# Inverse standard deviation of the normalisations: one power on GpSimd in place of ScalarE's square root and the vector engine's reciprocal

## The chip, the cores and the metric

The kernel runs on one core of one Trainium2 chip. The metric is the device time of the core in microseconds, lower is better. Before the change the median of three runs is 2083.49 us (2082.4 to 2088.18).

## The reference

The program is a decoder of four layers with three sublayers each: attention, cross attention and feed-forward, on 4 x 256 tokens of 256 channels. The twelve sublayers are all different in kind (chunked linear attention, grouped-query cross attention with rotary positions, ternary feed-forward, a state-space model, and so on). Every sublayer ends in the same residual sum and normalisation:

```python
def _layernorm(x, axis=-1, eps=1e-05):
    m = jnp.mean(x, axis=axis, keepdims=True)
    v = jnp.var(x, axis=axis, keepdims=True)
    return (x - m) / jnp.sqrt(v + eps)

x = _layernorm(x + _L0_attn_ref(x, ...), axis=-1)
x = _layernorm(x + _L0_xattn_ref(x, ctx_2048, ...), axis=-1)
x = _layernorm(x + _L0_ffn_ref(x, ...), axis=-1)
...                                # twelve in all
```

## The kernel before, in words

The 1024 tokens lie on 128 partitions in eight tiles of 256 channels (`NT` = 8): `Y` holds the sum before a normalisation, `X` the normalised tiles with tokens on partitions, `XT` the same turned, channels on partitions. Each sublayer is a row of stages. A stage (`stage`, line 172) is a block in which each engine runs its own list of instructions, joined by semaphores; at its end GpSimd clears the stage's semaphores and all engines meet at a barrier (lines 180 and 181). Nothing of the next stage runs before that.

Ten of the twelve normalisations are stages of their own (`layer_norm`, line 302). The statistics of each tile (`stats`) are there already. The vector engine makes mean and variance of the eight tiles (`mv`, line 321), adds the epsilon (line 323) and signals `ln_var`. ScalarE takes the square root of the eight variances of each partition (line 335) and signals `ln_std`. The vector engine takes the reciprocal (line 325) and normalises tile by tile (line 327). TensorE turns the tiles (line 349) in four groups, each after four normalised tiles, and ScalarE copies them to `XT` (line 339). At the start of the stage ScalarE takes a root of a constant into `ln_one` (line 333), and where its function table is not the one with the root, the table load stands ahead of that instruction.

Two normalisations are fused into the last stage of their sublayer, the quantised cross attention of the third layer (`quantized_core`) and the RWKV attention of the fourth (line 2298), by the class `Finish` (line 3223). It works in two halves of four tiles: `variance(half)`, `root(half)` on ScalarE (line 3275), `normalise(half)` with the reciprocal on the vector engine (line 3282), `turn(half)` on TensorE, `store(half)` on ScalarE. The order in which these stand among the stage's other work is written out by hand on each engine.

The head RMS (`head_rms`, line 558) also takes a square root on ScalarE (line 573); it is used in the first sublayer and twice in the cross attention of the second layer. In the RWKV sublayer the exponential of the time decay (line 2385) is the first thing that ScalarE does, and the vector engine's first scan (line 2432) needs it and TensorE's first product.

Of the kernel before, what the change touches and what calls it, by code (L numbers as in the profile page):

```python
# [18 lines left out]
P = 128  # L19
B, S, D = 4, 256, 256  # L20
TOK = B * S
NT = TOK // P
# [5 lines left out]
ALU = mybir.AluOpType  # L28
# [17 lines left out]
def rows(v):  # L46

    v = np.asarray(v).reshape(1, -1)
    return np.broadcast_to(v, (P, v.shape[1]))
# [68 lines left out]
def shape_constants():  # L118
    p, j = np.arange(P)[:, None], np.arange(P)[None, :]
    f = np.float32  # L120
    inv_freq = (f(1.0) / np.power(f(10000.0), np.arange(0, P, 2, dtype=f) / f(P))).astype(f)
    return dict(
        ident=(p == j).astype(f),
        keep=(p <= j).astype(f),
        deny_q=np.where(j > p, f(NEG), f(0)),
        deny_k=np.where(p > j, f(-NEG), f(0)),
        third=((p % 32 == np.arange(32)[None, :]) & (p < 96)).astype(f),
        eighth=(p // 16 == np.arange(8)[None, :]).astype(f),
        inv_freq=rows(inv_freq), ones=np.ones((P, P), f),
        rank=rows(np.arange(16, 0, -1).astype(f)))  # L130


def pack(parts):
# [168 lines left out]
def layer_norm(g, weights=None, out=None):  # L302
# [5 lines left out]
    with ExitStack() as ctx:  # L308
        sb, pb = places(g, ctx)
        st = g.stats  # L310
        mv = sb("ln_mv", [P, NT, 2])
        root_of_one = sb("ln_one", [P, 1])
        ps = [pb(f"ln_ps{i}", [P, 4, P]) for i in range(4)]
        with stage(g, "ln_var ln_std ln_chain ln_x ln_turned") as (
                block, var_ready, std_ready, chain_sem, x_ready, turned):

            @block.vector
            def _(dve):
                link = Count(dve, chain_sem)
                for t in range(NT):  # L320
                    last = nc.vector.bn_aggr(mv[:, t, :], st[:, t, :])
                link(last)
                nc.vector.tensor_scalar(mv[:, :, 1], mv[:, :, 1], LN_EPS, None, ALU.add).then_inc(var_ready, 1)
                dve.wait_ge(std_ready, 1)
                link(nc.vector.reciprocal(mv[:, :, 1], mv[:, :, 1]))  # L325
                for t in range(NT):
                    nc.vector.tensor_scalar(X[:, t, :], Y[:, t, :], mv[:, t, 0:1], mv[:, t, 1:2],  # L327
                                            ALU.subtract, ALU.mult).then_inc(x_ready, 1)

            @block.scalar  # L330
            def _(act):

                nc.scalar.activation(root_of_one[:, :], g.ones[:, 0:1], ACT.Sqrt)  # L333
                act.wait_ge(var_ready, 1)
                nc.scalar.activation(mv[:, :, 1], mv[:, :, 1], ACT.Sqrt).then_inc(std_ready, 1)  # L335
                if out is None:
                    for i in range(4):
                        act.wait_ge(turned, i + 1)
                        nc.scalar.copy(XT[:, i % 2, (i // 2) * 512:(i // 2) * 512 + 512],
                                       ps[i][:, :, :].rearrange("p a b -> p (a b)"))  # L340

            if out is None:
                @block.tensor
# [1539 lines left out]
def quantized_core(g, qT, kT, vi, sq, wp, ahead, weights):  # L1883
# [8 lines left out]
    with ExitStack() as ctx:  # L1892
# [8 lines left out]
        with stage(g, "qc_scored qc_max qc_bias qc_exp qc_turned0 qc_turned1 qc_turned2 qc_turned3 qc_turned4 qc_turned5 qc_used qc_recip "  # L1901
# [6 lines left out]
            @block.gpsimd  # L1908
            def _(pool):
                for i in range(ahead.count):  # L1910
                    ahead.compare(i, ahead_compared, ahead_made)
                pool.wait_ge(ahead_made, ahead.count)

            @block.sync
            def _(sp):
# [104 lines left out]
            def _(act):  # L2020
# [12 lines left out]
                                         scale=sq[:, t, h:h + 1], accum_out=sm[:, i:i + 1]).then_inc(exped, 1)  # L2033
                for t in range(NT):
                    store_turned(t)
                fin.root(0)
                fin.store(0)
                fin.root(1)
                fin.store(1)


# [256 lines left out]
def L3_attn(g, W, weights):  # L2298
# [8 lines left out]
    with ExitStack() as ctx:  # L2307
# [11 lines left out]
        with stage(g, "dm_kproduct dm_vrproduct dm_wexp dm_signs dm_highest dm_diff dm_arg dm_exps dm_vstored dm_gate "  # L2319
# [41 lines left out]
            def _(act):  # L2361
# [25 lines left out]
                for hf in range(2):  # L2387
# [2 lines left out]
                        store_v(hf, m)  # L2390
                    exponents(2 * hf + 1)
                    gates(hf)
                fin.root(0)
                fin.store(0)
                fin.root(1)
                fin.store(1)

            @block.gpsimd
            def _(pool):
# [7 lines left out]
                def weigh_before(u):  # L2407
                    pool.wait_ge(qsum, 2 * u + 2)
                    nc.gpsimd.tensor_tensor(eq[:, u], ea[:, u], before(q, u), ALU.mult).then_inc(before_weighted, 1)
# [6 lines left out]
                for hf in range(2):  # L2416
                    weigh(2 * hf)
                    weigh_before(2 * hf)
                    weigh(2 * hf + 1)
                    weigh_before(2 * hf + 1)  # L2420
                    weigh_gate(2 * hf)
                    weigh_gate(2 * hf + 1)

            @block.vector
            def _(dve):
# [797 lines left out]
class Finish:  # L3223
# [45 lines left out]

    def root(self, half):  # L3270

        nc = self.g.nc
        v = self.mv[:, 4 * half:4 * half + 4, 1]
        nc.scalar.wait_ge(self.var, half + 1)
        nc.scalar.activation(v, v, ACT.Sqrt).then_inc(self.std, 1)

    def normalise(self, half):

        nc, g, mv = self.g.nc, self.g, self.mv
        v = mv[:, 4 * half:4 * half + 4, 1]  # L3280
        nc.vector.wait_ge(self.std, half + 1)
        self.link(nc.vector.reciprocal(v, v))
        for t in range(4 * half, 4 * half + 4):
            nc.vector.tensor_scalar(g.X[:, t, :], g.Y[:, t, :], mv[:, t, 0:1], mv[:, t, 1:2], ALU.subtract,
                                    ALU.mult).then_inc(self.x, 1)
# [259 lines left out]
def program(nc, a, out, parts, spans, const_at, first=0, last=11):  # L3545
    g = Core()
    g.nc = nc
    with ExitStack() as ctx:
# [15 lines left out]
        g.inv_freq = const("inv_freq")  # L3564
        g.ones = const("ones")
        g.rank = const("rank")
        keep3 = sb("keep3", [P, 3, P])
        g.keep3 = keep3[:, :, :]
        ident_b = sb("ident_b", [P, P], BF16)
# [106 lines left out]
```

## Time and profile before

| | |
|---|---|
| median of 3 runs | 2083.49 us |
| profiled execution | 2080.46 us, span 2078.5 us |
| TensorE matmul busy | 1657.9 us, 80% of the span |
| vector engine busy | 1342.2 us, 65% |
| ScalarE busy | 1061.7 us, 51% |
| GpSimd busy | 575.4 us, 28% |
| mean granted TensorE clock | 0.863 |

The shares are averages over some fifty stages with different limits. In the normalisation stages no engine is busy with anything else, so they are read by their order in time, instruction by instruction. Times in the rows are microseconds from the start of the span.

### The profile page before, as it was taken

How to read it: one execution, taken by the hardware profiler on the slowest of the kernel's cores; microseconds unless marked ns; L12 is line 12 of the kernel's file. 1: busy time of each engine (PE TensorE's matmuls, PEld its weight loads, DVE VectorE, ACT ScalarE, POOL GpSimd, SP SyncE). 2: the span in 40 equal slices, each digit the busy share in tenths (PEclk: the TensorE clock that was granted, in tenths of full speed). 3: DMA queues.
4: the chain of work that ended last, by engine and by line, in shares of the span. 5: the costliest groups of instructions: out<-in, count | busy, mean ns of one | idle time of the engine just before them, and what ended most of it. 6: DMA issues, size and time to landing. Idle time of an engine off the chain costs nothing. (4 is left out here: it accounts for less than half of the span.)

```text
span 2078.5 us, 28504 instructions
## 1 busy us (share of the span) xinstructions
PE 1657.9 (80%) x9533; PEld 1039.9 (50%) x9541; DVE 1342.2 (65%) x2664; ACT 1061.7 (51%) x2191; POOL 575.4 (28%) x466
## 2 busy tenths in 40 slices
PE   7957999999997879998399579772899767457924
PEld 3743566666775536656266357451222434226712
DVE  4767777676664448883676456246999747825467
ACT  2024555565543248893188158324899621515525
POOL 0406341322100029890320000012990000406710
PEclk9989999999999989999699779896555669777958
DMA  4000000000001001110000000015999700020000
GB/s 199 27 1 26 1 1 1 1 1 1 1 1 43 16 32 42 51 41 16 0 2 2 26 1 2 23 77 136 162 182 184 123 21 5 0 81 1 2 0 21
DMA packets 163007, 80.65 MB, mean 39 GB/s; under 512 B 155280, under 2 KB 156432, under 8 KB 161200
## 3 DMA queue, kind: packets, MB, share of 16 engines
q1 hardware_dynamic: 162720, 78.46, 15.8%
q8 instruction: 77, 1.26, 0.3%
q14 instruction: 66, 0.54, 0.1%
q10 hardware_dynamic: 144, 0.39, 0.0%
HBM read 39.44 MB, written 1.11 MB: 20 GB/s over the span
## 5 line engine op out<-in xcount | busy, mean ns | idle before, releaser
L1213 POOL TENSOR_TENSOR ss_u<-dx,b_rows 128x512 f32<-128x512 f32 x128 | 159.0, 1273 | 242.3 <-POOLq L181 226.3
L2032 ACT ACTIVATE qc_p<-qc_s,qc_bias,sq 128x1024 int16<-128x1024 f32 x128 | 154.1, 1204 | 16.9 <-DVE qc_bias L1999 6.8
L1295 DVE TENSOR_TENSOR_SCAN ss_h<-ss_decay,ss_u 128x512 f32<-128x512 f32 x128 | 146.5, 1204 | 24.2 <-PE ss_ht L1253 18.4
L932 ACT ACTIVATE gq_p<-gq_s,gq_bias,gq_rq 128x512 f32<-128x512 f32 x128 | 98.5, 773 | 119.0 <-DVE gq_bias L1002 118.9
L1997 DVE TENSOR_REDUCE qc_mx<-qc_s 128x1 f32<-128x1024 f32 x128 | 155.4, 1214 | 3.8 <-PE qc_s L1932 3.8
L865 POOL TENSOR_TENSOR gq_xw<-gq_x,weights 128x512 f32<-128x512 f32 x48 | 67.9, 1414 | 295.1 <-ACT gq_x L892 294.5
L1932 PE MATMUL qc_s<-kT,qT 64*128 64x512 bf16 x256 | 130.8, 618 | 13.6 <-ACT qc_p L2032 7.3
L1267 PE MATMUL ss_acc<-ss_hc,consts 128*128 128x512 f32 x256 | 130.9, 594 | 0.0
L800 PE MATMUL gq_s<-gq_KT,gq_QT 128*128 128x512 f32 x256 | 121.5, 597 | 3.7 <-ACT gq_p L932 3.7
L822 PE MATMUL gq_o<-gq_pT,gq_V 128*128 128x256 f32 x512 | 121.2, 379 | 1.4 <-DVE gq_pT L1036 1.4
L999 DVE TENSOR_REDUCE gq_mx<-gq_s 128x1 f32<-128x512 f32 x128 | 88.3, 691 | 43.5 <-PE gq_s L800 43.1
L822 PEld LDWEIGHTS gq_o<-gq_pT,gq_V 128*128 128x128 f32 x512 | 94.2, 190 | 24.3 <-issue 12.5
L1253 PEld LDWEIGHTS ss_ht<-consts,ss_h 128*128 128x128 f32 x512 | 64.7, 143 | 79.4 <-issue 52.8
L1036 DVE COPY gq_pT<-gq_t 128x512 f32<-128x512 f32 x64 | 44.3, 692 | 86.6 <-PE gq_t L810 86.6
L1223 ACT ACTIVATE ss_decay<-delta,ss_A 128x510 f32<-128x510 f32 x128 | 87.8, 686 | 16.7 <-DVE ss_h L1295 15.7
L349 PE MATMUL ln_ps<-consts,X 128*128 128x128 f32 x144 | 32.7, 420 | 79.2 <-DVE X L327 79.2
L779 PE MATMUL gq_item<-weights,XT 128*128 128x512 f32 x192 | 91.4, 597 | 4.2 <-ACT gq_x L892 2.1
L1231 ACT ACTIVATE ss_hc<-ss_ht,bct 128x512 f32<-128x512 f32 x128 | 86.8, 678 | 7.8 <-PE ss_ht L1253 7.6
L1942 PEld LDWEIGHTS qc_o<-vi,qc_pT 128*128 128x128 f16 x1024 | 37.8, 106 | 105.9 <-issue 65.2
L1472 ACT ACTIVATE bc_w<-bc_s 128x512 f32<-128x512 f32 x128 | 72.4, 597 | 32.3 <-PE bc_s L1413 30.5
L1253 PE MATMUL ss_ht<-consts,ss_h 128*128 128x128 f32 x512 | 78.1, 276 | 12.2 <-DVE ss_h L1295 11.7
L3442 POOL MEMSET qi_ks<- 128x512 bf16 x2 | 1.0, 524 | 299.9 <-POOLq L181 299.9
(576 smaller groups left out, 4127.1 us busy)
## 6 DMA issues: line engine op xcount, KB each, us to landing
b_rows<-b_rows SPq DMA_DIRECT2D x16, 512.0 KB, 3.6
weights<-in_weights SPq DMA_DIRECT2D x1, 6152.0 KB, 17.7
weights<-in_weights SPq DMA_DIRECT2D x1, 5248.0 KB, 16.7
weights<-in_weights SPq DMA_DIRECT2D x1, 3072.0 KB, 10.4
weights<-in_weights SPq DMA_DIRECT2D x1, 2156.0 KB, 7.4
qc_pT<-qc_p SPq DMA_TRANSPOSE x128, 3.3
weights<-in_weights SPq DMA_DIRECT2D x1, 1410.0 KB, 9.0
weights<-in_weights SPq DMA_DIRECT2D x1, 1282.0 KB, 6.2
```

The lines of the kernel that those rows point to most:

```text
L779: last = nc.tensor.matmul(pj[:, :], src[:, k, t * P:t * P + P], w[:, k, :], start=(k == 0), stop=(k == 1))
L800: nc.tensor.matmul(sc[t][:, :], QT[:, u, t * P:t * P + P], KT[b % 2][:, u // 4, :], start=True, stop=True).then_inc(scored, 1)
L822: last = nc.tensor.matmul(po[:, :], V[b % 2][:, k, u // 4 * P:u // 4 * P + P], prT[c % 2][:, k, :], start=(k == 0), stop=(k == 3))
L932: nc.scalar.activation(pr[c % 2][:, t, :], sc[t][:, :], ACT.Exp, bias=bias[:, c, t:t + 1], scale=rq[b % 2][:, t, u:u + 1], accum_out=sm[:, ...
L999: nc.vector.tensor_reduce(mx[:, c, t:t + 1], sc[t][:, :], AX.X, ALU.max, negate=True).then_inc(maxed, 1)
L1213: nc.gpsimd.tensor_tensor(u_in[i % 3][:, :], dx[:, m, hf * HT:hf * HT + HT], rows.rows[c % 2][:, n % rows.NEACH, :], ALU.mult).then_inc(in ...
L1253: last = nc.tensor.transpose(ht[k % 2][:, m * P:m * P + P], h[group % 2][:, m, t * P:t * P + P], g.ident)
L1267: nc.tensor.matmul(acc[t][:, :], g.ident, hc[k % 3][:, :], start=False, stop=(n == NS - 1)).then_inc(summed, 1)
L1295: nc.vector.tensor_tensor_scan(h[group % 2][:, m, :], decay[i % 2][:].rearrange("p b t -> p (b t)"), u_in[i % 3][:, :], 0.0, ALU.mult, ALU ...
L1932: last = nc.tensor.matmul(sc[u % 3][:, n * 512:n * 512 + 512], qT[e, t, h // 2, :], kT[e, 4 * n:4 * n + 4, h // 2, :], start=True, stop=True)
L1997: nc.vector.tensor_reduce(mx[:, i:i + 1], sc[i % 3][:, :], AX.X, ALU.max, negate=True).then_inc(maxed, 1)
L2032: nc.scalar.activation(pi[i % R][:, :], sc[i % 3][:, :], ACT.Exp, bias=bias[:, i:i + 1], scale=sq[:, t, h:h + 1], accum_out=sm[:, i:i + 1] ...
```

## The change

The root and the reciprocal are replaced by one instruction on GpSimd: the variances to the power of a constant -0.5, which is a new column of the constants. ScalarE's dummy root and its root go, and so do the reciprocals of the normalisations. In the two fused normalisations the root moves to GpSimd's list.

```diff
@@ shape_constants
-        rank=rows(np.arange(16, 0, -1).astype(f)))
+        rank=rows(np.arange(16, 0, -1).astype(f)), neg_half=np.full((P, 1), -0.5, f))
@@ layer_norm
                 dve.wait_ge(std_ready, 1)
-                link(nc.vector.reciprocal(mv[:, :, 1], mv[:, :, 1]))
                 for t in range(NT):
...
             @block.scalar
             def _(act):
-
-                nc.scalar.activation(root_of_one[:, :], g.ones[:, 0:1], ACT.Sqrt)
-                act.wait_ge(var_ready, 1)
-                nc.scalar.activation(mv[:, :, 1], mv[:, :, 1], ACT.Sqrt).then_inc(std_ready, 1)
...
+            @block.gpsimd
+            def _(pool):
+                pool.wait_ge(var_ready, 1)
+                nc.gpsimd.tensor_tensor(mv[:, :, 1], mv[:, :, 1], g.neg_half.to_broadcast([P, NT]),
+                                        ALU.pow).then_inc(std_ready, 1)
@@ quantized_core, GpSimd
                 pool.wait_ge(ahead_made, ahead.count)
+                fin.root(0)
+                fin.root(1)
@@ quantized_core and the RWKV attention, ScalarE
-                fin.root(0)
                 fin.store(0)
-                fin.root(1)
                 fin.store(1)
@@ the RWKV attention, GpSimd
                     weigh_before(2 * hf + 1)
+                    if hf == 1:
+                        fin.root(0)
                     weigh_gate(2 * hf)
                     weigh_gate(2 * hf + 1)
+                fin.root(1)
@@ Finish
     def root(self, half):
...
-        nc.scalar.wait_ge(self.var, half + 1)
-        nc.scalar.activation(v, v, ACT.Sqrt).then_inc(self.std, 1)
+        nc.gpsimd.wait_ge(self.var, half + 1)
+        nc.gpsimd.tensor_tensor(v, v, g.neg_half.to_broadcast([P, 4]), ALU.pow).then_inc(self.std, 1)
     def normalise(self, half):
...
-        self.link(nc.vector.reciprocal(v, v))
```

ScalarE at the second normalisation (behind the grouped-query cross attention of the first layer), before; `ln_mv` holds mean and variance, `ln_ps` the turned tiles:

```order
L330 UNCONDITIONAL_BRANCH
L333 ACT_TABLE_LOAD
L333 ACTIVATE ln_one<-consts 128x1
L335 ACTIVATE ln_mv<-ln_mv 128x8
L339 COPY XT<-ln_ps_132 128x512
```

The same place after, on ScalarE:

```order
L328 UNCONDITIONAL_BRANCH
L333 COPY XT<-ln_ps_130 128x512
L333 COPY XT<-ln_ps_131 128x512
L333 COPY XT<-ln_ps_132 128x512
L333 COPY XT<-ln_ps_133 128x512
```

And on GpSimd, which had only its semaphore clears there:

```order
L180 ISA x29
L336 UNCONDITIONAL_BRANCH
L339 TENSOR_TENSOR ln_mv<-ln_mv,consts 128x8
L177 UNCONDITIONAL_BRANCH
L180 ISA x13
```

The table load, the dummy root and the root are gone from ScalarE; the power stands alone on GpSimd.

ScalarE at the start of the RWKV attention, before (`dm_w` is the exponential of the time decay, `dm_d` a difference that the vector engine makes):

```order
L2360 UNCONDITIONAL_BRANCH
L2385 ACT_TABLE_LOAD
L2385 ACTIVATE dm_w<-weights 128x2
L2377 ACTIVATE dm_arg_476<-dm_d,dm_wn 128x512
L2378 ACTIVATE dm_a_467<-dm_arg_476 128x512
```

And after:

```order
L2360 UNCONDITIONAL_BRANCH
L2385 ACTIVATE dm_w<-weights 128x2
L2377 ACTIVATE dm_arg_468<-dm_d,dm_wn 128x512
L2378 ACTIVATE dm_a_459<-dm_arg_468 128x512
```

The load ahead of the exponential is gone, since the table of the exponential is still in place from the sublayers before.

GpSimd in the second half of the RWKV attention, before (`dm_no` is the numerator, `dm_r` the gate):

```order
L2403 TENSOR_TENSOR dm_bv<-dm_b_468,dm_v 128x512
L2405 TENSOR_TENSOR dm_v<-dm_eb,dm_v 128x512
L2409 TENSOR_TENSOR dm_eq<-dm_ea,dm_q 128x512
L2414 TENSOR_TENSOR dm_no<-dm_no,dm_r 128x512 x2
L177 UNCONDITIONAL_BRANCH
```

And after, with the two powers (`fi_mv`):

```order
L2401 TENSOR_TENSOR dm_bv<-dm_b_460,dm_v 128x512
L2403 TENSOR_TENSOR dm_v<-dm_eb,dm_v 128x512
L2407 TENSOR_TENSOR dm_eq<-dm_ea,dm_q 128x512
L3276 TENSOR_TENSOR fi_mv<-fi_mv,consts 128x4
L2412 TENSOR_TENSOR dm_no<-dm_no,dm_r 128x512 x2
L3276 TENSOR_TENSOR fi_mv<-fi_mv,consts 128x4
```

The first power stands ahead of the two gate products, the second behind them. Over the whole program ScalarE has 39 table loads before and 28 after: twelve go (six of line 333, two of line 3275, and those of lines 1585, 1856, 2032 and 2385), and one comes, ahead of the root of the first head RMS in the second layer's cross attention (line 573).

## Rows read from the trace of the kernel before

**Rows 1.** The waits of all engines: us in total, times, longest.

```profile
PE ln_ps L349 <- DVE X L327: 79.2, 9, 30.6
```

**Rows 2.** Order of time, normalisation without table load: start, us, engine, what.

```profile
149.77 0.17 DVE L323 TENSOR_SCALAR ln_mv<-ln_mv 128x8 f32<-128x8 f32 x1
...
150.46 2.67 DVE L327 TENSOR_SCALAR X<-Y,ln_mv 128x256 f32<-128x256 f32 x8
```

**Rows 3.** Order of time, normalisation with table load.

```profile
650.44 1.28 ACT L333 ACT_TABLE_LOAD   x1 [5.77 <-PEq L181]
...
651.15 0.17 DVE L323 TENSOR_SCALAR ln_mv<-ln_mv 128x8 f32<-128x8 f32 x1
651.74 0.20 ACT L333 ACTIVATE ln_one<-consts 128x1 f32<-128x1 f32 x1
...
652.31 2.67 DVE L327 TENSOR_SCALAR X<-Y,ln_mv 128x256 f32<-128x256 f32 x8
```

**Rows 4.** Line 333 on ScalarE: ns min, median, max, first and last start.

```profile
L333 ACT ACTIVATE ln_one<-consts x10: 202/203/203, 149.1 to 2071.2; 128x1 f32<-128x1 f32 x10
L333 ACT ACT_TABLE_LOAD  x6: 1283/1283/1283, 650.4 to 2069.9; - x6
```

**Rows 5.** GpSimd's groups (busy us, mean ns of one), then its first two-input instruction.

```profile
L1213 POOL TENSOR_TENSOR ss_u<-dx,b_rows 128x512 f32<-128x512 f32 x128 | 159.0, 1273 | 242.3 <-POOLq L181 226.3 <-DVE ss_h L1295 16.0
...
L2629 POOL TENSOR_TENSOR mn_h<-mn_h,weights 128x256 f32<-128x256 f32 x8 | 5.7, 748 | 27.1 <-ACT mn_sq L2635 27.1
...
L3443 POOL TENSOR_TENSOR X<-X,weights 128x2048 f32<-128x2048 f32 x1 | 3.8, 3811 | 0.0
...
L3668 POOL MEMSET const-float32-1.0<- 128x1 f32 x1 | 0.1, 98 | 0.0
...
159.54 1.09 POOL L865 TENSOR_TENSOR gq_xw<-gq_x,weights 128x512 f32<-128x512 f32 x1 [67.81 <-ACT gq_x L892]
```

**Rows 6.** Order of time, RWKV attention: hand-overs from and to GpSimd.

```profile
1771.19 1.27 POOL L2403 TENSOR_TENSOR dm_bv<-dm_b,dm_v 128x512 f32<-128x512 f32 x1 [211.11 <-ACT dm_v L2366]
...
1772.50 3.27 DVE L2444 TENSOR_TENSOR_SCAN dm_p<-dm_a,dm_bv 128x256 f32<-128x256 f32 x2 [3.10 <-POOL dm_bv L2403]
...
1783.61 0.69 DVE L2452 TENSOR_TENSOR dm_no<-dm_no,dm_v 128x512 f32<-128x512 f32 x1
...
1784.45 1.58 POOL L2414 TENSOR_TENSOR dm_no<-dm_no,dm_r 128x512 f32<-128x512 f32 x1 [3.90 <-DVE dm_no L2452]
```

**Rows 7.** Order of time, first half of the normalisation in the quantised attention.

```profile
1650.62 0.17 DVE L3268 TENSOR_SCALAR fi_mv<-fi_mv 128x4 f32<-128x4 f32 x1
...
1651.69 0.42 DVE L365 BATCH_NORM_STATS2 stats<-Y 128x6 f32<-128x256 f32 x1
...
1653.24 1.38 DVE L3284 TENSOR_SCALAR X<-Y,fi_mv 128x256 f32<-128x256 f32 x4
```

**Rows 8.** Order of time, first half of the normalisation in the RWKV attention.

```profile
1813.43 3.35 DVE L2455 RECIPROCAL dm_eq<-dm_eq 128x512 f32<-128x512 f32 x1
1816.82 0.18 DVE L3282 RECIPROCAL fi_mv<-fi_mv 128x4 f32<-128x4 f32 x1
```

**Rows 9.** Order of time, its second half.

```profile
1831.86 0.17 DVE L3268 TENSOR_SCALAR fi_mv<-fi_mv 128x4 f32<-128x4 f32 x1
...
1832.52 1.38 DVE L3284 TENSOR_SCALAR X<-Y,fi_mv 128x256 f32<-128x256 f32 x4
```

**Rows 10.** Order of time, start of the RWKV attention.

```profile
1761.25 1.28 ACT L2385 ACT_TABLE_LOAD   x1 [0.85 <-PEq L181]
...
1761.29 2.81 PE L2334 MATMUL dm_k<-XT,weights 128*128 128x512 f32 x6 [1.51 <-PEq L181]
...
1763.35 1.26 DVE L2432 TENSOR_TENSOR_SCAN dm_o<-dm_w,dm_k 128x256 f32<-128x256 f32 x2
```

**Rows 11.** Order of time, first head RMS of the second layer's cross attention.

```profile
1002.42 2.56 ACT L571 ACTIVATE rms_sq<-q 128x256 f32<-128x256 f32 x8 [1.87 <-PEq L181]
...
1005.94 0.42 ACT L573 ACTIVATE rms_ms<-rms_ms 128x256 f32<-128x256 f32 x1 [0.96 <-DVE rms_ms L583]
```

**Rows 12.** Order of time, ScalarE's first exponential in the quantised attention, behind its load.

```profile
1458.89 1.20 ACT L2032 ACTIVATE qc_p<-qc_s,qc_bias,sq 128x1024 int16<-128x1024 f32 x1 [1.31 <-DVE qc_bias L1999]
```

More of the change, by code:

```diff
@@ L311, in layer_norm @@
         mv = sb("ln_mv", [P, NT, 2])
-        root_of_one = sb("ln_one", [P, 1])
         ps = [pb(f"ln_ps{i}", [P, 4, P]) for i in range(4)]
@@ L2392, in _ @@
                     gates(hf)
-                fin.root(0)
                 fin.store(0)
-                fin.root(1)
                 fin.store(1)
@@ L3270, in root @@
     def root(self, half):
-        nc = self.g.nc
+        nc, g = self.g.nc, self.g
         v = self.mv[:, 4 * half:4 * half + 4, 1]
-        nc.scalar.wait_ge(self.var, half + 1)
-        nc.scalar.activation(v, v, ACT.Sqrt).then_inc(self.std, 1)
+        nc.gpsimd.wait_ge(self.var, half + 1)
+        nc.gpsimd.tensor_tensor(v, v, g.neg_half.to_broadcast([P, 4]), ALU.pow).then_inc(self.std, 1)
     def normalise(self, half):
@@ L3566, in program @@
         g.rank = const("rank")
+        g.neg_half = const("neg_half")
         keep3 = sb("keep3", [P, 3, P])
```

## The prediction

> **What bounds the kernel now.** I read four views in this order. First the waits: TensorE waits 79.2 us in nine standing-alone normalisations for the normalised tiles X [rows 1]. Nothing else runs in such a stage, so every tenth of a microsecond between the variance and the first normalise instruction is a tenth of the total. Second the order of time inside such a stage. Without a table load, the vector engine adds the epsilon from 149.77 to 149.94, ScalarE takes the root, the vector engine the reciprocal, and the first normalise starts at 150.46: a gap of 0.52 us [rows 2]. With a table load, the load runs from 650.44 to 651.72, the dummy root follows at 651.74, and the gap from 651.32 (end of the epsilon add) to 652.31 is 0.99 us [rows 3]: the load starts with the stage, and all but 0.47 us of it and of the dummy root lies beside the bn_aggr work. Six of the ten stages have the load [rows 4], four have not. Third the GpSimd rows, for the price of what replaces the pair [rows 5], and the hand-overs from and to GpSimd [rows 6]. Fourth the places where a table load stood or will stand outside these stages [rows 7 to 12].
>
> **The change, term by term.** Let G be the new gap: hand-over to GpSimd, one pow, hand-over back. GpSimd starts 0.15 us after the vector instruction it waits for (1784.30 to 1784.45), and the vector engine 0.04 us after GpSimd (1772.46 to 1772.50) [rows 6]. So G = pow + 0.19.
>
> 1. Ten standing-alone stages: 10 G - (4 x 0.52 + 6 x 0.99) = 10 G - 8.02 us [rows 2 to 4].
> 2. The second half of each fused normalisation, where the engines wait in the same way: 1831.86 + 0.17 = 1832.03 to 1832.52 is 0.49 us, and the other one is the same in kind: 2 G - 0.98 us [rows 9].
> 3. The first half in the quantised attention: the epsilon add ends at 1650.79, ScalarE first finishes copies, then loads the table, and the normalise starts at 1653.24, 2.45 us later. The vector engine has adds and statistics of its own until 1651.69 + 0.42 = 1652.11 [rows 7]. With the pow it starts at 1652.14 if G is under 1.35: -1.10 us. TensorE has the turn of these tiles and then the last projection behind it, so it is on the path. If G is over 1.35 the gain shrinks by the difference. GpSimd's own list there is comparisons of the next sublayer's weights, with the two roots behind them.
> 4. The first half in the RWKV sublayer: the vector engine computes a quotient meanwhile and reaches its small reciprocal at 1816.82, straight from a reciprocal of 3.35 us of that quotient. Only the small one goes: 0.18 + 0.03 = -0.21 us [rows 8]. On GpSimd the gate products are now queued behind the root, which waits for the variance. They need the numerator, for which the vector engine has two instructions of 0.69 us behind the variance [rows 6], so a pow of up to about 1.2 us holds nothing up, and a dearer one still has the 3.35 us as slack. I cost it at nothing.
> 5. Start of the RWKV sublayer: ScalarE's exponential table need not be loaded again, since nothing has displaced it. The load runs from 1761.25 and the vector engine waits for the exponential behind it, so that its first scan starts at 1763.35. TensorE's first product is two matmuls of a row of six in 2.81 us, so there by about 1762.3; the scan can then start at about 1762.35: -1.00 us, between -1.28 (the whole load) and 0 (if ScalarE's later chain absorbs it) [rows 10].
> 6. One load is added: the first head RMS of the second layer's cross attention found the root table in place and now doesn't. Its squares end at 1004.98, its root starts at 1005.94; a load of 1.28 us set off at 1004.98 ends at 1006.26: +0.33 us, between 0 and +1.28 [rows 11].
> 7. Loads at three other stage starts go too. ScalarE waits 1.31 us for the vector engine behind one of them [rows 12]; I cost all three at nothing, since what covers them is the first scores and maxima of the stage; without that cover they would be worth up to 1.28 us each.
> 8. The constants grow by one column of 760; I cost it at nothing.
>
> Sum: 12 G - 8.02 - 0.98 - 1.10 - 0.21 - 1.00 + 0.33 = 12 G - 10.98 us. Break-even is G = 0.915, a pow of 0.73 us.
>
> **The price of the pow.** The trace has no pow on any engine. From below: the shortest GpSimd row of all, a memset of one column, 0.10 us; then G = 0.29 and the sum is -7.5 us. A multiply costs 748 ns for 256 columns and 1273 ns for 512, that is 2.05 ns a column over a fixed 0.22 us, so eight columns at a multiply's price are 0.24 us, G = 0.43, sum -5.8 us [rows 5]. From above: the dearest GpSimd row, 3.81 us; G = 4.0, sum +37.0, and +39.7 with the 2.65 us that term 3 loses. I take the row nearest in kind and size, the two-input operation on 256 columns: 0.75 us. That leaves 0.53 us for eight columns of pow above the fixed part; that is 66 ns a column, some thirty times a multiply; nothing in the trace supports this figure more closely, so both ends stay in the range. G = 0.94 and the sum is +0.3 us. The profiled execution took 2080.46 us and would take 2080.8; it lies 3.03 us under the median of the three runs, and carried over to that median the forecast is 2083.8 us.
>
> **Two rules weighed.** The load costs 1.28 us here and the next activation starts 0.02 us behind it [rows 3]. The Trainium skill (ScalarE: Activation LUTs, What ACT_TABLE_LOAD costs) charges a drain of 1.38 us on top, 2.66 us for each switch. By that rule eleven loads fewer would be worth some 29 us (an estimate from that page), and the forecast would be 2055; the trace does not agree, because no such drain follows the load and most loads are covered.
>
> The first two-input instruction on GpSimd of the whole program, at 159.54, takes 1.09 us, less than the 1.27 us of a later group of the same shape, so no first use shows in this trace [rows 5]. The Trainium skill (GPSIMD Engine Reference, Instruction dispatch) says that the first call into a freshly loaded library kernel costs about 6 us without an instruction to show for it. If pow were such a kernel, the first normalisation would carry it once and the forecast would be 6 us later (an estimate from that page). No run here shows it so far.
>
> **The rivals.**
> - *Cheap pow.* The pow costs less than 0.4 us; at a multiply's price the sum is -5.8 us, 2077.7, at the floor -7.5 us, 2076.0. For it: the operand is eight columns. Against it: pow is no multiply; on the vector engine a reciprocal of 512 columns is 3.35 us where other two-input work on it is 0.69 [rows 6, 8], so division-like functions cost several times the plain ones even there.
> - *Dear pow, the rival on the other side.* A new wait takes the place of the removed one: in all ten stages and both second halves, the vector engine, and TensorE behind it, wait for GpSimd. It decides from G = 0.915, and passes 0.3% (6.25 us) from G = 1.43, a pow of 1.24 us. At a pow of 1.8 us the sum is 12 x 2.0 - 10.98 + 0.65 = +13.7 us, 2097.2; at the dearest GpSimd row 2123.2. For it: nothing in the trace bounds a transcendental function on this engine, and none of its rows is one. Against it: its rows here of 1 to 512 columns take 0.10 to 1.58 us [rows 5, 6].
> - *The covered loads were on the path after all.* With the three of term 7 in full, 3 x 1.28 = 3.8 us more gain: 2080.0. Against it: ScalarE's wait behind the load [rows 12].
> - *A first pow that is dear once.* The first normalisation waits for it, at the most as long as the dearest GpSimd row, 3.81 us: 2087.6. For it: pow stands nowhere in the program before. Against it: the first multiply's 1.09 us [rows 5].
> - *The change does nothing it says.* Against it: the order of ScalarE's instructions in the changed kernel has 28 table loads for 39, and no root in a normalisation.
>
> **How the numbers follow.** 0.3% is about what a measurement of this kernel tells from no change. Pow between 0.4 and 1.24 us, sum from -3.9 to +6.2: 0.53. Cheap pow: 0.20, of which 0.14 beyond 0.3%. Dear pow: 0.24, half of it over +22 us. Covered loads on the path: 0.02. A first pow dear once: 0.01. So faster 0.14, same 0.53 + 0.06 + 0.02 + 0.01 = 0.62, slower 0.24. The range runs from the floor of the pow, 2083.5 - 7.5 = 2076, to a G of 2.7 (12 x 2.7 - 10.98 + 1.35 = +22.8), 2106; half of the dear case and little else is left out.
>
> **What would show it.** In the profile after: ten pow rows of eight columns and four of four; their mean is the whole question, and the gap between the epsilon add and the first normalise should be that mean plus 0.19. All ten stages should have the same gap, where they now have 0.52 or 0.99. In the quantised attention the first normalise should follow the statistics directly at 0.03 us; the RWKV sublayer's first scan should come 1.0 us earlier after the stage's start; the head RMS should show a load that ends 0.3 us late. I am wrong in size if the mean pow is outside 0.4 to 1.24 us, and wrong in mechanism if the gap in a stage differs from pow plus 0.19 by over 0.2 us, or if stages without a normalisation change by over 1 us.

## The result: the changed kernel is 1.1% slower, beyond the range

| | before | after |
|---|---|---|
| median (range) of 4 runs each on one chip | 2085.84 us (2082.40 to 2088.18) | 2108.92 us (2104.58 to 2109.90) |
| profiled execution, its span | 2080.46, 2078.5 us | 2109.90, 2108.0 us |
| mean granted TensorE clock | 0.863 | 0.852 |

The ratio after to before is 1.0108, with an interval of 1.0085 to 1.0131. By the medians that is 23.1 us. The forecast was 2083.8, and the time lies 2.9 us above the top of the range. Three of the kernels below each have one execution far outside the rest (2409, 3399 and 4307 us); the ratios leave it out, the medians keep it and move by less than 0.2 us.

**The price of the power.** The groups of the two tiles in the changed kernel (engine, operation, count, then the shortest, median and longest in ns, first and last start):

```profile
L322 DVE TENSOR_SCALAR ln_mv<-ln_mv x10: 171/172/173, 153.5 to 2099.4; 128x8 f32<-128x8 f32 x10
L339 POOL TENSOR_TENSOR ln_mv<-ln_mv,consts x10: 1634/1637/1667, 153.8 to 2099.6; 128x8 f32<-128x8 f32 x10
...
L3276 POOL TENSOR_TENSOR fi_mv<-fi_mv,consts x4: 1007/1026/1389, 1671.5 to 1853.0; 128x4 f32<-128x4 f32 x4
```

Eight columns take 1.64 us and four 1.01 us: about 0.16 us a column over a fixed 0.4 us. The forecast had taken 0.75 us for eight. The wait of TensorE for the normalised tiles, 79.2 us before [rows 1], is now

```profile
PE ln_ps L349 <- DVE X L325: 88.3, 9, 31.8
```

The same stage as in [rows 3], in order of time after the change:

```profile
658.16 0.17 DVE L322 TENSOR_SCALAR ln_mv<-ln_mv 128x8 f32<-128x8 f32 x1
658.41 1.67 POOL L339 TENSOR_TENSOR ln_mv<-ln_mv,consts 128x8 f32<-128x8 f32 x1 [115.18 <-DVE ln_mv L322]
660.11 2.67 DVE L325 TENSOR_SCALAR X<-Y,ln_mv 128x256 f32<-128x256 f32 x8 [1.78 <-POOL ln_mv L339]
```

The gap is 1.78 us where it was 0.99; it is 1.75 to 1.78 us in all ten stages, against 0.52 or 0.99 before. Over the ten stages that adds 17.6 - 8.0 = 9.6 us. This is well short of 23.1 us.

**Where a large part of the rest went.** The third normalisation and the first product of the stage behind it show it. `ln_ps` are the sixteen turns of the normalised tiles, `si_x` the projection that follows, and ScalarE's line 3144 (3145 after) the first to read what it makes, its first consumer. Before, in order of time:

```profile
699.64 2.67 DVE L327 TENSOR_SCALAR X<-Y,ln_mv 128x256 f32<-128x256 f32 x8
701.08 3.67 PE L349 MATMUL ln_ps<-consts,X 128*128 128x128 f32 x16 [5.03 <-DVE X L327]
...
706.26 4.10 PE L3084 MATMUL si_x<-XT,weights 128*128 128x512 f32 x9 [1.51 <-PEq L181]
708.25 0.69 ACT L3144 ACTIVATE xc<-si_x,weights 128x512 f32<-128x512 f32 x1 [2.88 <-PE si_x L3084]
```

After:

```profile
708.40 2.68 DVE L325 TENSOR_SCALAR X<-Y,ln_mv 128x256 f32<-128x256 f32 x8 [1.75 <-POOL ln_mv L339]
709.83 3.68 PE L349 MATMUL ln_ps<-consts,X 128*128 128x128 f32 x16 [6.26 <-DVE X L325]
...
715.03 5.28 PE L3085 MATMUL si_x<-XT,weights 128*128 128x512 f32 x7 [1.52 <-PEq L181]
718.82 0.69 ACT L3145 ACTIVATE xc<-si_x,weights 128x512 f32<-128x512 f32 x1 [4.69 <-PE si_x L3085]
```

The turns take 3.67 us in both, and both stages need 5.2 us from the first turn to the first matmul behind. But the same product then takes 1.99 us before and 3.79 us after. The windows cut at these times (length, busy time of TensorE with its instructions, granted clock as a share of full speed, DMA share, GB/s), first before, then after:

```profile
706.26:708.25 1.99, 1.99 (x5) 1.00 0.49 107
```

```profile
715.03:718.82 3.79, 3.79 (x5) 0.50 0.65 207
```

The same five matmul records run at 2.4 GHz before and at 1.2 GHz after. TensorE had stood still before the turns for 5.03 us before and 6.26 us after; in these rows nothing else about its work differs. The Trainium skill (TensorE: Matmul & The Clock Gate, HAM oscillation) describes bursts of matmuls parted by waits that start again at the lower clock, at a price of half the throttled time. The trace agrees in size: 1.80 us of 3.79.

I read this time, from the first matmul behind a normalisation to its first consumer, in the eight stages where it can be told, in every kernel that follows. It is 1.99 to 2.08 us at the full clock and 3.4 to 3.9 at the lower one (the fourth stage has a shorter product, 1.14 or 2.08). The ninth is 2.58 us in every profile, and behind the tenth there is nothing. I call a product at the lower clock a slow product. Before, one of the eight is slow (the fifth, 3.46 us); after, seven (all but the second): 3.79, 1.99, 3.79, 2.08, 3.79, 3.70, 3.86 and 3.62 us. The eight add up to 9.9 us more than before.

### The profile page after: what moved, and what is told of

Its sections match the earlier page's. It is cut to its first block and busy times, and to the rows that moved or that the text cites. A ratio compares the mean times of both kernels' runs of the same rounds, so it can differ in the third digit from the quotient of the medians.

```text
span 2108.0 us, 28469 instructions
## 1 busy us (share of the span) xinstructions
PE 1677.4 (80%) x9533; PEld 1047.9 (50%) x9541; DVE 1338.9 (64%) x2650; ACT 1043.4 (49%) x2156; POOL 596.2 (28%) x480
## 3 DMA queue, kind: packets, MB, share of 16 engines
q8 instruction: 78, 1.28, 0.2%
## 5 line engine op out<-in xcount | busy, mean ns | idle before, releaser
L339 POOL TENSOR_TENSOR ln_mv<-ln_mv,consts 128x8 f32<-128x8 f32 x10 | 16.4, 1644 | 724.1 <-DVE ln_mv L322 724.1
L2034 ACT ACTIVATE qc_p<-qc_s,qc_bias,sq 128x1024 int16<-128x1024 f32 x128 | 154.2, 1204 | 21.5 <-DVE qc_bias L2001 11.4
L333 ACT COPY XT<-ln_ps 128x512 f32<-128x512 f32 x36 | 21.1, 586 | 139.1 <-PE ln_ps L349 139.1
## 6 DMA issues: line engine op xcount, KB each, us to landing
weights<-in_weights SPq DMA_DIRECT2D x1, 5248.0 KB, 16.7
```

The costliest lines, as they stand in the source:

```text
L2034: nc.scalar.activation(pi[i % R][:, :], sc[i % 3][:, :], ACT.Exp, bias=bias[:, i:i + 1], scale=sq[:, t, h:h + 1], accum_out=sm[:, i:i + 1] ...
```

## The experiments

In all of them theory A is that the longer standstill of TensorE leaves the stage behind at the lower clock. Its rivals were that the tiles or the constants had moved (B), that the new order of the queues or the absent table loads cost (C), and that the gaps alone account for the time (D). The texts of expectation speak of nine products; of these, eight can be told apart. The number after each ratio is the change of the median against the runs of the kernel before on the same chip.

**const_only.** The kernel before with the new column of the constants, which nothing reads.

```diff
-        rank=rows(np.arange(16, 0, -1).astype(f)))
+        rank=rows(np.arange(16, 0, -1).astype(f)), neg_half=np.full((P, 1), -0.5, f))
```

> The kernel before with the extra column of constants alone; nothing reads it, and all that follows it lies 32 bytes further on. Theory A (what is lost beyond the sum of the gaps is TensorE's granted clock behind longer pauses): same as before, 2083 to 2088 us. Rival B (the move of the tiles, or the larger load of constants, costs time of itself): up to 15 us slower, about 2100, with the first projection behind 36 us late by 1.5 us as in the changed kernel.

Measured 2083.77 us, ratio 0.9999 (0.9984 to 1.0014), -0.4 us; one slow product of eight. The constants cost nothing, and B falls as far as they go.

**cheap_mult.** The kernel after with everything where the change puts it, but the power is a multiply of the same size; the inverse deviation is left out and a constant stands for it.

```diff
-                nc.gpsimd.tensor_tensor(mv[:, :, 1], mv[:, :, 1], g.neg_half.to_broadcast([P, NT]),
-                                        ALU.pow).then_inc(std_ready, 1)
+                nc.gpsimd.tensor_tensor(mv[:, :, 1], g.ones[:, 0:NT], g.neg_half.to_broadcast([P, NT]),
+                                        ALU.mult).then_inc(std_ready, 1)
```

> The changed kernel with the power replaced by a multiply of two constants on the same 8 or 4 columns, so the standard deviation is left out of the result (a constant -0.5 takes its place); every wait, queue and removed table load is that of the change. It shows what the change would be worth if the power were cheap. By the sum of my prediction (multiply 0.24 us, gap 0.43) -5.8 us, 2077 to 2080. Theory A: at or below that, with the clock back at 0.86. Rival C (the moved order on the queues or the absent table loads cost the time, not the power's length): it stays near 2100 to 2108.

Measured 2078.20 us, ratio 0.9969 (0.9955 to 0.9982), -5.9 us; two slow products. Its row for the instruction:

```profile
L339 POOL TENSOR_TENSOR ln_mv<-consts x10: 200/202/204, 151.7 to 2069.2; 128x8 f32<-128x8 f32 x10
```

With 0.20 us the gap is 0.32 us. The forecast's sum at a multiply's price was -5.8 us, and that the two agree is in part luck: at the measured gap the sum is 12 x 0.32 - 10.98 = -7.1 us, and 1.0 us of it, the load at the RWKV start, was never to be had (term 5 below). Tiles, constants, queues and loads are all as in the kernel after, so B and C fall: the whole loss hangs on how long the power takes.

**paused and paused_mid.** The kernel before, root and reciprocal in place. In the ten normalisation stages the vector engine also waits for an addition of 690 (400) columns on GpSimd that starts with the variance.

```diff
+            @block.gpsimd
+            def _(pool):
+                pool.wait_ge(var_ready, 1)
+                nc.gpsimd.tensor_tensor(filler[:, :], ...[:, 0:690], ...[:, 0:690], ALU.add).then_inc(filled, 1)
...
                 link(nc.vector.reciprocal(mv[:, :, 1], mv[:, :, 1]))
+                dve.wait_ge(filled, 1)
```

> The kernel before, whole and with its table loads, but in the ten normalisation stages the vector engine also waits for a GpSimd addition of 690 columns (about 1.64 us by 2.05 ns a column over 0.22) that starts when the variance is there, so that the gap is about 1.8 us as in the changed kernel. Gaps alone: 10 x 1.8 - 8.0 = +10 us, 2095. Theory A (longer pauses also cost clock in the stage behind): +20 to +30 us, 2104 to 2112. Rival D (the extra loss belongs to something else in the change): +10 us, no more.

> The kernel before, paused as in the longer one but by an addition of 400 columns, about 1.04 us, so that the gap in all ten normalisation stages is about 1.24 us (0.52 or 0.99 before, 1.83 in the longer pause). Gaps alone: 10 x 1.24 - 8.0 = +4.4 us, 2088. Theory A (the clock behind the stage depends on the pause): between +4 and +14 us, with three to seven of the nine first products behind a normalisation slow (3.4 to 3.8 us to the first copy instead of 2.0). Rival D (gaps alone): 2088, with two of nine slow as before.

The filler of 690 columns is as long as the power:

```profile
L321 POOL TENSOR_TENSOR ln_filler<-Y x10: 1636/1637/1639, 152.1 to 2096.4; 128x690 f32<-128x690 f32 x10
```

paused: 2105.00 us, ratio 1.0094 (1.0071 to 1.0117), +20.9 us, seven slow products. Its gaps are 1.83 us, so they add 18.3 - 8.0 = 10.3 us by themselves. paused_mid: 2098.89 us, ratio 1.0070 (1.0050 to 1.0090), +15.1 us, four slow products; its gaps of 1.22 us add 4.2 us. The second is 1 us above what theory A had allowed it (+4 to +14). D falls: both lose some 11 us more than their gaps. In the profile of paused the eight first products hold 9.7 us of that. In the profile of paused_mid they hold only 4.9 of 10.9 us, so there more than half is not located. The third stage's product in paused, with the same columns of the windows as above:

```profile
715.98:719.77 3.79, 3.79 (x5) 0.50 0.66 210
```

No power, no absent load and no new column is in this kernel. The wait alone makes most of the loss of the kernel after (20.9 of 23.1 us).

**after_warm and before_warm.** TensorE turns the identity into a spare buffer twelve times at the start of the normalisation stages, once in the kernel after and once in the kernel before. The nine stages in which TensorE has turns are concerned.

```diff
                 def _(pe):
+                    for j in range(12):
+                        nc.tensor.transpose(spare[:, j % 4, :], g.ident, g.ident)
```

> The changed kernel, and in each normalisation stage TensorE turns the identity twelve times into a spare bank before it waits for the normalised tiles, so that it is busy for 1.3 to 2.6 us of the pause. Theory A: the granted clock behind the normalisations is high and 10 to 20 us come back, 2088 to 2098. Rival D: no change, 2105 to 2110, or slower by what the twelve overshoot.

> The kernel before with the twelve turns of the identity on TensorE at the start of each normalisation stage. Theory A: the two of nine slow first products of the kernel before become fast and the turns inside the stages run faster, 5 to 12 us gain, 2072 to 2079. Rival: the clock is high enough there already and the turns overshoot, 2084 to 2088.

after_warm: 2089.96 us, ratio 1.0021 (1.0008 to 1.0033), +5.8 us, two slow products; the gaps are still 1.75 to 1.78 us. before_warm: 2076.93 us, ratio 0.9972 (0.9956 to 0.9988), -6.8 us, no slow product. It is the fastest of all kernels here. Its third normalisation:

```profile
695.76 1.15 PE L347 MATMUL ln_spare<-consts 128*128 128x128 f32 x9
...
698.21 1.09 PE L352 MATMUL ln_ps<-consts,X 128*128 128x128 f32 x8 [1.30 <-DVE X L328]
...
699.50 1.09 PE L352 MATMUL ln_ps<-consts,X 128*128 128x128 f32 x8 [0.20 <-DVE X L328]
```

Each half of the turns now runs in 1.09 us, where all sixteen took 3.67 at the lower clock. From the first normalise instruction to the first matmul of the next stage it takes 5.39 us for 6.62. Turns faster than at the lower clock are found in five of the nine stages of after_warm and eight of before_warm, and this is a gain that the kernel before had to get as well. So the extra turns do not only undo what the change did, and the fair comparison is between the two warm kernels: the change costs 5.8 + 6.8 = 12.7 us there by the medians (10.2 by the ratios), against 23.1 (22.5) without the turns. So some 10 to 12 us of the loss exist only without those turns; the intervals of the three ratios leave this uncertain by some 6 us.

**split_pow.** The kernel after, with mean, epsilon and power in two halves of four tiles, so that the first power runs beside the second half of the means.

```diff
+                for hf in range(2):
+                    for t in range(4 * hf, 4 * hf + 4):
+                        last = nc.vector.bn_aggr(mv[:, t, :], st[:, t, :])
+                    link(last)
+                    v = mv[:, 4 * hf:4 * hf + 4, 1]
+                    nc.vector.tensor_scalar(v, v, LN_EPS, None, ALU.add).then_inc(var_ready, 1)
                 for t in range(NT):
+                    if t % 4 == 0:
+                        dve.wait_ge(std_ready, t // 4 + 1)
```

> The changed kernel, but in the ten normalisation stages mean, variance and power go in two halves of four tiles, so that the first power starts after four aggregations and takes about 1.0 us instead of 1.64. The last aggregation lies beside it. Gap from the end of all aggregations to the first normalise about 0.5 us instead of 1.77; the pause of TensorE is 1.2 us shorter. Gaps alone against the changed kernel: -12 us, 2096. Theory A: clock comes back as well, 2080 to 2092. Rival D: 2096.

Measured 2086.01 us, ratio 1.0008 (0.9994 to 1.0021), +2.2 us; two slow products. From the last of the epsilon additions to the first normalise instruction it is 0.63 to 0.67 us. Its second normalisation:

```profile
650.26 0.38 DVE L321 BATCH_NORM_AGGREGATE ln_mv<-stats 128x2 f32<-128x6 f32 x4 [2.64 <-PEq L181]
...
650.93 2.17 POOL L346 TENSOR_TENSOR ln_mv<-ln_mv,consts 128x4 f32<-128x4 f32 x2 [114.72 <-DVE ln_mv L324]
...
652.00 1.38 DVE L328 TENSOR_SCALAR X<-Y,ln_mv 128x256 f32<-128x256 f32 x4 [0.66 <-POOL ln_mv L346]
```

The power still costs 2 x 1.0 us, but one of them lies beside work, and nearly all of the loss is gone.

**split_warm and before_warm20.** Ten turns in split_pow, and twenty in place of twelve in the kernel before.

```diff
+                    for j in range(10):          # split_warm; range(20) in before_warm20
+                        nc.tensor.transpose(spare[:, j % 4, :], g.ident, g.ident)
```

> The changed kernel with mean, variance and power in two halves, and ten turns of the identity on TensorE at the start of each normalisation stage. Split alone gave 2086 with two of nine first products slow. Theory A: those two and the turns inside the stages become fast, 2070 to 2078, at or under the kernel before with its twelve turns (2077). Rival: the turns overshoot the shorter pause and give nothing, 2084 to 2088.

> The kernel before with twenty turns of the identity instead of twelve. With the clock high they take 2.2 us, with it low 4.3 us, against a pause of 2.8 to 3.3 us inside the stage. Theory A allows a small further gain where the clock is high (2074 to 2077) and a loss where it is low, up to 1 us a stage (2085).

split_warm: 2086.75 us, ratio 1.0021 (1.0008 to 1.0033), +4.2 us; it missed its expectation. Ten turns left the normalisation's own turns slow in the eight stages (6.38 to 6.64 us from the first normalise to the next stage's first matmul; 5.39 where they are fast), so they bought nothing; only one product of eight was slow. Its profile also begins with a slow stretch at 38 us, ahead of any normalisation. before_warm20: 2081.13 us, ratio 0.9999 (0.9986 to 1.0012), -1.5 us, no slow product. In its third stage the twenty turns run on until 700.9 us:

```profile
696.95 3.98 PE L347 MATMUL ln_spare<-consts 128*128 128x128 f32 x20 [2.23 <-PEq L181]
700.77 1.91 PE L352 MATMUL ln_ps<-consts,X 128*128 128x128 f32 x16
```

The normalisation's sixteen turns stand behind them in one block, where before_warm had started the first eight as soon as four tiles were there. By the same reading as for before_warm (normalisation stages and the products behind them) the twenty turns gain 8.3 us where the twelve gain 10.5, so their late end accounts for 2.2 of the 5.3 us between the two; where the rest is isn't shown.

**fused_only.** The kernel before with only the two fused normalisations changed (the lines of the diff in `Finish`, `quantized_core` and the RWKV attention).

```diff
-        nc.scalar.activation(v, v, ACT.Sqrt).then_inc(self.std, 1)
+        nc.gpsimd.tensor_tensor(v, v, g.neg_half.to_broadcast([P, 4]), ALU.pow).then_inc(self.std, 1)
...
-        self.link(nc.vector.reciprocal(v, v))
```

> The two fused normalisations changed (powers on GpSimd), the ten standing-alone stages as before. By the rows of the changed kernel: the first half in the quantised attention starts 1.2 us earlier, both second halves wait 0.65 us longer each, the rest cancels: 0 +- 1 us. Theory A: 2081 to 2086, same as before, since no long pause of TensorE is added. Rival C (the order on the GpSimd queue in the fused stages costs time): over 2090.

Measured 2083.81 us, ratio 1.0008 (0.9996 to 1.0020), +1.2 us. The loss is in the ten stages that stand alone. One thing speaks against reading too much into a single trace: this one has four slow products, though the code of its standing-alone stages is that of the kernel before. (The eighth has one table load more, since the quantised attention no longer takes a root, and a gap of 0.99 us for 0.52; its product is one of the four.) The profile is of an execution of 2087.26 us, the second longest of ten.

**pow_sizes.** Powers and multiplies of several sizes on GpSimd, behind the last normalisation.

```diff
+                    for op, ns in ((ALU.pow, (1, 2, 4, 8, 16, 32, 64, 128)), (ALU.mult, (1, 8, 32, 128))):
+                        for n in ns:
+                            nc.gpsimd.tensor_tensor(probe[:, n0:n0 + n], g.ones[:, 0:n],
+                                                    g.neg_half.to_broadcast([P, n]), op)
```

> The changed kernel with eight powers of 1 to 128 columns and four multiplies of 1 to 128 columns on GpSimd behind the last normalisation, for their durations. From 1.01 us at 4 columns and 1.64 at 8: 0.16 us a column over 0.39 us, so 20 us at 128 columns, if the price is linear; a multiply about 0.2 us at 1 to 8 columns. The rival reading is a fixed price with steps, under 5 us at 128.

One execution, 2141.70 us. The group (shortest, median, longest in ns):

```profile
L346 POOL TENSOR_TENSOR ln_probe<-consts x12: 183/1044/20719, 2094.3 to 2138.4; 128x1 f32<-128x1 f32 x2, 128x8 f32<-128x8 f32 x2, 128x32 f32<-128x32 f32 x2, 128x128 f32<-128x128 f32 x2
```

The longest, 20.72 us, is the power of 128 columns: (20.72 - 1.64) / 120 = 0.16 us a column, as between four and eight. The base was one here and the variance in the kernel, so the price does not hang on the data as far as these two go.

Up to its last normalisation the code of pow_sizes is that of the kernel after but for one spare tile, so its profile is a second look at that kernel. Six of its eight products are slow, and they are not the same ones: the third and the fifth are fast there, the second is slow. Its second stage, ahead of the feed-forward's first product (`ff_ps`):

```profile
659.66 3.67 PE L357 MATMUL ln_ps<-consts,X 128*128 128x128 f32 x16 [8.55 <-DVE X L326]
...
664.85 19.38 PE L1138 MATMUL ff_ps<-XT,weights 128*128 128x512 f32 x40 [1.52 <-PEq L181]
...
668.64 0.60 ACT L1148 ACTIVATE ff_r<-ff_ps 128x512 f32<-128x512 f32 x1 [4.69 <-PE ff_ps L1138]
```

TensorE stands still for 8.55 us before the turns, as in the kernel after. There the product took 1.99 us, here 3.79.

## Why the prediction was wrong, point by point

The time by the forecast's own sum with what was measured, in us of the profiled executions:

| step | forecast | measured |
|---|---|---|
| price of eight columns of pow | 0.75 (0.10 to 3.81) | 1.64 |
| hand-overs | 0.19 | 0.12 |
| 1: ten stages | 10 G - 8.02 = +1.4 | +9.6 |
| 2: second halves, fused | 2 G - 0.98 = +0.9 | +1.3 |
| 3: first half, quantised | -1.10 | -1.22 |
| 4: first half, RWKV | -0.21 | -0.22 |
| 5: load at the RWKV start | -1.00 | 0 |
| 6: load ahead of the head RMS | +0.33 | +0.34 |
| 7, 8: covered loads, constants | 0 | 0 |
| TensorE's clock behind the stages | not there | +9.9 |

Without the last row the measured terms make +9.8 us, and the time would have been some 2093 us, inside the range. **Two steps failed.** The first is the price of the pow, a term that was mis-sized. The forecast went by the nearest row in kind and size and ended at 66 ns a column where 157 were measured; it had called this figure weakly supported, and the dear rival (chance 0.24) stated this part rightly, the wait for GpSimd and its sign. The second weighs more, and no rival had it: "12 G" priced a longer gap at one microsecond per microsecond, and the clock of TensorE behind it at nothing. In the kernel before TensorE's turns already run at 1.2 GHz, but in seven of eight stages the clock is back at 2.4 GHz as the next stage begins. With 0.8 to 1.2 us more of standstill it is, in most stages, back only about the end of the first product, and that product costs up to 1.8 us more. At a pow of 1.8 us the forecast said 2097.2; the runs gave 2108.9 at 1.64. Of its three signs of being wrong two came true: the mean pow lies outside 0.4 to 1.24 us, and stages without a normalisation changed by over 1 us. A third step, term 5, failed by 1.0 us (below).

**Hand-overs and gaps.** GpSimd starts 0.08 us after the epsilon addition and the vector engine 0.03 us after GpSimd. The gap is the pow plus 0.12, within the 0.2 us that the prediction set for its mechanism, and alike in all ten stages, as it said.

**Term 2.** The last half of the RWKV attention after the change, which answers to [rows 9]:

```profile
1852.78 0.17 DVE L3269 TENSOR_SCALAR fi_mv<-fi_mv 128x4 f32<-128x4 f32 x1
1853.03 1.01 POOL L3276 TENSOR_TENSOR fi_mv<-fi_mv,consts 128x4 f32<-128x4 f32 x1 [10.57 <-DVE fi_mv L3269]
1854.07 1.38 DVE L3284 TENSOR_SCALAR X<-Y,fi_mv 128x256 f32<-128x256 f32 x4 [1.12 <-POOL fi_mv L3276]
```

A gap of 1.12 us for 0.49. The term took the price of eight columns for four, which would have been too much at the true price.

**Term 3** was right. The quantised attention after the change, which answers to [rows 7]:

```profile
1671.47 1.03 POOL L3276 TENSOR_TENSOR fi_mv<-fi_mv,consts 128x4 f32<-128x4 f32 x1 [90.41 <-DVE fi_mv L3269]
...
1672.22 0.42 DVE L365 BATCH_NORM_STATS2 stats<-Y 128x6 f32<-128x256 f32 x1
1672.55 0.72 DVE L3284 TENSOR_SCALAR X<-Y,fi_mv 128x256 f32<-128x256 f32 x2
```

From the start of the last statistics to the first normalise it is 0.33 us, and was 1.55. The power is done at 1672.50, just in time.

**Term 4** was right too. The instructions that answer to [rows 6, 8]:

```profile
1832.75 1.39 POOL L3276 TENSOR_TENSOR fi_mv<-fi_mv,consts 128x4 f32<-128x4 f32 x1 [6.51 <-DVE fi_mv L3269]
1833.31 0.69 DVE L2453 TENSOR_TENSOR dm_no<-dm_no,dm_v 128x512 f32<-128x512 f32 x1
...
1834.15 1.58 POOL L2412 TENSOR_TENSOR dm_no<-dm_no,dm_r 128x512 f32<-128x512 f32 x1
1834.64 3.35 DVE L2456 RECIPROCAL dm_eq<-dm_eq 128x512 f32<-128x512 f32 x1
1838.03 1.38 DVE L3284 TENSOR_SCALAR X<-Y,fi_mv 128x256 f32<-128x256 f32 x4
```

The gate product starts 0.15 us after its numerator, as before, so the power ahead of it on GpSimd holds nothing up. The normalise follows the quotient's reciprocal by 3.39 us for 3.61.

**Term 5** failed by its reading of [rows 10]. It took two matmuls of a row of six for the whole first product. In cheap_mult, which has no such load and TensorE at the full clock there, the scan still starts 2.07 us after the first matmul:

```profile
1756.11 3.24 PE L2334 MATMUL dm_k<-XT,weights 128*128 128x512 f32 x7 [1.49 <-PEq L181]
1758.18 1.26 DVE L2433 TENSOR_TENSOR_SCAN dm_o<-dm_w,dm_k 128x256 f32<-128x256 f32 x2 [1.34 <-PE dm_k L2334]
```

With the load it was 1763.35 - 1761.29 = 2.06 us. The product came no sooner than the exponential, and the load was hidden. In the kernel after the scan starts 3.62 us after the first matmul, and waits for TensorE:

```profile
1780.97 5.22 PE L2334 MATMUL dm_k<-XT,weights 128*128 128x512 f32 x8 [1.52 <-PEq L181]
...
1784.59 1.26 DVE L2433 TENSOR_TENSOR_SCAN dm_o<-dm_w,dm_k 128x256 f32<-128x256 f32 x2 [2.88 <-PE dm_k L2334]
```

**Term 6** was right. Squares, load and root, which answer to [rows 11]:

```profile
1015.98 2.56 ACT L571 ACTIVATE rms_sq<-q 128x256 f32<-128x256 f32 x8 [1.86 <-PEq L181]
1018.55 1.28 ACT L573 ACT_TABLE_LOAD   x1
...
1019.84 0.42 ACT L573 ACTIVATE rms_ms<-rms_ms 128x256 f32<-128x256 f32 x1
```

From the first square to the root it is 3.86 us for 3.52. The load costs its 1.28 us and the root starts 0.01 us behind it. The rule of the Trainium skill that the prediction weighed (ScalarE: Activation LUTs, What ACT_TABLE_LOAD costs), 2.66 us a switch with a drain, is not borne out here either.

**Term 7** was right. The first exponential of the quantised attention [rows 12] stands behind a load before:

```profile
1456.34 1.86 PE L1932 MATMUL qc_s<-kT,qT 64*128 64x512 bf16 x6 [3.05 <-PEq L181]
```

And after, without the load:

```profile
1477.30 1.86 PE L1934 MATMUL qc_s<-kT,qT 64*128 64x512 bf16 x6 [3.06 <-PEq L181]
...
1479.85 1.21 ACT L2034 ACTIVATE qc_p<-qc_s,qc_bias,sq 128x1024 int16<-128x1024 f32 x1 [6.28 <-DVE qc_bias L2001]
```

From the first matmul to the exponential it is 2.55 us in both, so the rival that had the covered loads on the path falls for this load. The other two show no gain either: in one stage the vector engine starts its products 1.82 us after its first instruction in both kernels (1183.11 to 1184.93, 1199.88 to 1201.70), in the other ScalarE had waited 2.71 us for the vector engine behind the load.

**The first pow** is as long as the others to 0.03 us (the longest of ten is 1.667), so that rival falls.

**How full the account is.** By the medians 23.1 us were lost; 9.8 from the terms and 9.9 from the first products leave 3.4 us. (The kernel before was run again beside the experiments, 21 to 25 times on each of three chips, with medians of 2082.6 to 2084.1 us where the four runs of the table have 2085.8, so what is left may be 5 to 7 us.) The spans of the two profiled executions differ by 29.5 us, since that of before was a short one. In them 3.75 us arise ahead of the first changed instruction, where the same differences come and go between kernels that are alike there (the first epsilon addition lies at 149.8 us before, at 149.4 in const_only, 151.8 in paused, 154.2 in paused_mid). Some 6 us more lie further behind. 3.7 of them are between the ninth and the tenth normalisation, where a stretch of 50.42 us at a granted clock of 0.90 became 54.14 us at 0.85; 2.5 are between the eighth and the ninth, where const_only shows them too. The two warm kernels check the account only roughly: 9.8 us of terms, two slow products of 1.8 us and the turns inside the stages, which are slow in three stages more of after_warm and cost 3.3 us there, make 16.7; measured were 12.7 (10.2 by the ratios).

**What stays open.** The length of a standstill alone makes no rule over the stages: the second stage has TensorE idle for 7.76 us before and 8.55 after, the longest of the eight, and its product is fast in both, while the third's is slow at 6.26. Which stage comes out slow in an execution isn't settled: in pow_sizes the second is slow at the same 8.55 us, and the third fast at 6.27. cheap_mult has two slow products with shorter gaps than the kernel before, which has one, and fused_only has four; paused has a fast one where the kernel after has a slow one. The share of slow products follows the gaps only roughly: one or two of eight up to a gap of 0.99 us (fused_only apart), four at 1.22 and six or seven from 1.75 on (after_warm, with its turns, has two). Each is one profile; the medians carry the verdicts. Nor is it settled why before_warm gains 6.8 us where its normalisation stages and the products behind them show 10.5 us less than before, nor where paused_mid loses the 6 us beyond gaps and first products, and split_warm its 4.2.

## What to carry to other kernels

Price a wait in a stage in which TensorE stands still by two numbers: the wait, and the clock that TensorE is granted in the first product behind it, read from windows cut at that product. Here 0.8 to 1.2 us more of wait cost up to 1.8 us on top, a power on GpSimd was nearly free only where other work ran beside it (no kernel with it was faster than the one before), and twelve idle turns on TensorE that end before its real ones gained 6.8 us, where twenty gained nothing that the runs can tell.

## What the runs showed of the hardware

- GpSimd's power takes about 0.16 us a column over a fixed 0.4 us (1.01 us at 4 columns, 1.64 at 8, 20.72 at 128). A multiply of 4 or 8 columns takes 0.20 us (cheap_mult).
- An addition of 690 columns takes 1.64 us on GpSimd, as long as the power of eight.
- A power of four columns took 1.39 us in the RWKV attention, where the vector engine ran two-input work of 0.69 us beside it, and 1.01 to 1.03 us elsewhere. In cheap_mult the multiply of four columns in that place took 0.59 us, and 0.20 in the other three.
- Sixteen turns take 3.67 us at 1.2 GHz and 2 x 1.09 us at 2.4 GHz. In the kernel before all nine stages take 3.46 to 3.68 us for them; TensorE stands still for 4.97 to 7.76 us before them, and for 30.58 us in the ninth.
- A power on GpSimd had no first-use cost: 1.63 to 1.67 us, the first of them too.
